# Four quarter transposes for one, and K, Q and V loads issued from POOL instead of SP

## What is computed

```python
def fc(x, z, r):                      # Poincare-ball layer, c = 1
    lam = 2.0 / (1.0 - sum(x * x, -1))
    zn = norm(z, axis=0)
    v = 2 * zn * arcsinh(lam * (x @ (z / zn)) * cosh(2 * r) - (lam - 1) * sinh(2 * r))
    w = sinh(v)
    return w / (1 + sqrt(1 + sum(w * w, -1)))

def attn(x):                          # 16 heads of 64
    Q, K, V = fc(x, z_q, b_q), fc(x, z_k, b_k), x @ w_v.T + b_v
    return softmax(Q @ K.T / 8) @ V   # per head, 2048 x 2048

def ffn(x):
    xp = shift_by_one_token(x)
    xr, xk = mu_r * x + (1 - mu_r) * xp, mu_k * x + (1 - mu_k) * xp
    return sigmoid(xr @ W_r.T) * (relu(xk @ W_k.T) ** 2 @ W_v.T)

x = x + layernorm(attn(layernorm(x)))
x = x + layernorm(ffn(layernorm(x)))
```

## Time and profile before

| | |
|---|---|
| time, median of 2 runs | 3289.42 us (3283.85 to 3295.0) |
| the profiled execution | 3304.93 us, span 3303.1 us on core 2 |
| PE busy | 1878.3 us (57%) |
| ACT busy | 1684.9 us (51%) |
| DVE busy | 1453.6 us (44%) |
| POOL busy | 163.0 us (5%) |
| DMA transposes | 40, all on SP, median 6.7 us from issue to landing |
| K, Q and V loads in attention | 192, all on SP |

### The profile page before, as it was taken

One profiled execution on the slowest core, in us unless ns is written; L12 is line 12 of the kernel. 1 busy time (PEld: TensorE's weight loads), 2 busy tenths in 40 slices (PEclk: granted clock), 3 DMA queues, 4 the chain that ended last, 5 costly groups with the idle time before them and its releaser, 6 DMA issues.

```text
span 3303.1 us, 27750 instructions; the slowest of 8 cores (3266.8 to 3303.1 us)
## 1 busy us (share of the span) xinstructions
PE 1878.3 (57%) x7360; PEld 559.8 (17%) x7360; DVE 1453.6 (44%) x2455; ACT 1684.9 (51%) x1721; POOL 163.0 (5%) x256
## 2 busy tenths in 40 slices
PE   0272462277777787770507354416777978878614
PEld 0130120011122121120203121101111212212101
DVE  2255554211544636527434555440145273363474
ACT  0144645477666766751102653656777467466410
POOL 0000011000000000000000011010000000000000
PEclk9985786589899899895758776668987877878856
DMA  5512123522413314312252122063232142241111
GB/s 75 120 51 45 36 48 59 110 71 53 100 44 88 89 30 109 82 28 51 36 118 74 35 58 51 19 109 80 61 84 69 39 112 55 54 120 47 43 35 39
DMA packets 321561, 217.08 MB, mean 66 GB/s; under 512 B 271872, under 2 KB 280320, under 8 KB 321408
## 3 DMA queue, kind: packets, MB, share of 16 engines
q1 hardware_dynamic: 283264, 109.86, 15.0%
q0 software_dynamic: 38144, 105.45, 13.2%
HBM read 169.03 MB, written 42.21 MB: 64 GB/s over the span
## 4 chain that ended last, share of the span: by engine, by line
ACT 33%; PE 28%; DVE 21%; DMA 9%; issue 7%; DVEq 1%; ACTq 1%; SPq 0%; POOL 0%; POOLq 0%
ACT pool L1095 18%; PE p_attA L1039 4%; DMA pool<-pool 4%; PE psc L1070 3%; PE psc L942 3%; PE p_attB L1047 3%; PE psc L641 3%; PE psc L917 3%; PE psc L678 3%; DVE dump L371 2%; DVE dump L368 2%; ACT pool L533 2%; ACT pool L536 2%; ACT pool L506 2%; ACT pool L509 2%
## 5 line engine op out<-in xcount | busy, mean ns | idle before, releaser
L1095 ACT ACTIVATE pool<-psc 128x1024 bf16<-128x1024 f32 x1024 | 1048.9, 1024 | 538.3 <-PE psc L1077 469.9
L1039 PE MATMUL p_attA<-pool 128*128 128x512 bf16 x1024 | 434.4, 424 | 377.8 <-ACT pool L1095 212.9
L1070 PE MATMUL psc<-pool 64*128 64x512 bf16 x1024 | 428.7, 429 | 46.8 <-DMA pool<-s_vaug 46.8
L1047 PE MATMUL p_attB<-pool 128*128 128x512 bf16 x1024 | 441.7, 431 | 0.0
L1077 PE MATMUL psc<-pool 64*128 64x512 bf16 x1024 | 428.6, 429 | 0.0
L1100 DVE CAST pool<-p_attA 1x512 bf16<-1x512 f32 x64 | 43.8, 685 | 824.8 <-PE p_attB L1047 803.8
L678 PE MATMUL psc<-w_sb,pool 128*128 128x512 bf16 x512 | 141.5, 441 | 287.4 <-DVE pool L693 287.4
L892 PE MATMUL psc<-pool,w_sb 128*128 128x512 bf16 x512 | 128.1, 410 | 190.5 <-DVE pool L877 185.9
L1039 PEld LDWEIGHTS p_attA<-pool 128*128 128x128 bf16 x1024 | 99.6, 97 | 714.6 <-issue 714.6
L457 PE MATMUL psc<-dump,ones_bf 128*128 128x512 bf16 x64 | 35.0, 572 | 286.9 <-DVE dump L451 286.9
L1070 PEld LDWEIGHTS psc<-pool 64*128 64x128 bf16 x1024 | 91.3, 94 | 540.4 <-issue 540.4
(11 more groups left out here) (129 smaller groups left out, 2437.4 us busy)
## 6 DMA issues: line engine op xcount, KB each, us to landing
pool<-s_vaug SPq DMA_DIRECT2D x64, 520.0 KB, 5.1
pool<-s_kfm SPq DMA_DIRECT2D x64, 512.0 KB, 3.4
pool<-x POOLq DMA_DIRECT2D x8, 2048.0 KB, 8.6
pool<-x POOLq DMA_DIRECT2D x32, 512.0 KB, 3.6
out<-pool POOLq DMA_DIRECT2D x32, 512.0 KB, 3.0
s_vaug<-pool POOLq DMA_DIRECT2D x32, 260.0 KB, 2.3
s_qfm<-pool POOLq DMA_DIRECT2D x32, 256.0 KB, 4.8
s_kfm<-pool POOLq DMA_DIRECT2D x32, 256.0 KB, 4.6
```

What stands on the lines that cost most here:

```text
L1039: T(lambda t, c=c, po=po, vof=vof: t.matmul(p_attA[:, :], vsl[:, vof:vof + 128], PT[:, po:po + 512], start=(c == 0), stop=(c == 15), skip_ ...
L1047: tk = T(lambda t, c=c, po=po, vof=vof: t.matmul(p_attB[:, :], vsl[:, vof + 65:vof + 193], PT[:, po + 512:po + 1024], start=(c == 0), stop ...
L1070: T(lambda t, kof=kof, qof=qof, reg=reg: t.matmul(psc[:, reg:reg + 512], Ksl[0:64, kof:kof + 128], Qsl[0:64, qof:qof + QB], start=True, st ...
L1095: lambda s, reg=reg, po=po: s.activation(PT[:, po:po + 1024], psc[:, reg:reg + 1024], AF.Exp, scale=0.125),
```

## The change

Each big DMA transpose is issued as four, one for each tile of 128 tokens (1024 columns of the source). In the production head and in `emit_bndC` each quarter waits for its own normalised tile; the others wait for what the one transpose waited for. The transpose of the denominators is issued as four of 128 columns. Readers wait for the last of the four, as they waited for the one. The three loads of `emit_loads` are emitted with `G` (POOL) instead of `Y` (SP), with the same waits, semaphores and place in the program.

```diff
--- before.py
+++ after.py
@@ -431,11 +431,15 @@
                     ALU.mult, ALU.add),
                     waits=[tk_ln, pc.get("xtm_free_%d" % par)], inc=1))
             tS_ln = p.last["s"]
-            tk_xf_all = Y(lambda y, xnf=xnf, xntm=xntm:
-                          y.dma_start_transpose(
-                r3(xnf[:, :]), r3(xntm[:, :])),
-                waits=[tk_xn[3], pc["xnf_free"][par]], inc=16,
-                sem="y_xp")
+            tk_xf = []
+            for tt in range(4):
+                tk_xf.append(Y(lambda y, tt=tt, xnf=xnf, xntm=xntm:
+                               y.dma_start_transpose(
+                    r3(xnf[:, tt * D:(tt + 1) * D]),
+                    r3(xntm[:, tt * D:(tt + 1) * D])),
+                    waits=[tk_xn[tt], pc["xnf_free"][par]], inc=16,
+                    sem="y_xp"))
+            tk_xf_all = tk_xf[-1]
             pc["xtm_free_%d" % par] = tk_xf_all
             return {"xf_all": tk_xf_all, "par": par, "base": base,
                     "xnf": xnf, "tk_xn3": tk_xn[3], "tS_ln": tS_ln}
@@ -769,18 +773,23 @@
                 waits=[("g_rc", p.cnt["g_rc"]), cy.get("rcp")],
                 inc=16, sem="y_dn")
             cy["dn"] = tk_dn
-            tk_xa = Y(lambda y, afm=attn_fm2[bnd["qb"] % 2]:
-                      y.dma_start_transpose(
-                r3(attn_tm[:, :]), r3(afm[:, :])),
-                waits=[bnd["evac7"], cy["x1stt"], cy["of_free"]],
-                inc=16, sem="y_xp")
-            cy["afm_free"][bnd["qb"] % 2] = tk_xa
-            tk_dt = Y(lambda y: y.dma_start_transpose(
-                den_tm[:, :].rearrange("p (b t) -> p b t", t=16),
-                den_sb[0:16, :].rearrange("p (b t) -> p b t", t=128)),
-                waits=[tk_dn], inc=16, sem="y_xp")
-            bnd["xa"] = tk_xa
-            bnd["dt"] = tk_dt
+            tk_xa = []
+            for tt in range(4):
+                tk_xa.append(Y(lambda y, tt=tt, afm=attn_fm2[bnd["qb"] % 2]:
+                               y.dma_start_transpose(
+                    r3(attn_tm[:, tt * D:(tt + 1) * D]),
+                    r3(afm[:, tt * D:(tt + 1) * D])),
+                    waits=[bnd["evac7"], cy["x1stt"], cy["of_free"]],
+                    inc=16, sem="y_xp"))
+            cy["afm_free"][bnd["qb"] % 2] = tk_xa[-1]
+            tk_dt = []
+            for tt in range(4):
+                tk_dt.append(Y(lambda y, tt=tt: y.dma_start_transpose(
+                    den_tm[:, tt * 16:(tt + 1) * 16],
+                    den_sb[0:16, tt * 128:(tt + 1) * 128]),
+                    waits=[tk_dn], inc=16, sem="y_xp"))
+            bnd["xa"] = tk_xa[-1]
+            bnd["dt"] = tk_dt[-1]
 
         def emit_bndA_v(bnd):
             tk_rcp = V(lambda v: v.reciprocal(rc_tm[:], den_tm[:]),
@@ -834,11 +843,14 @@
                     lncol("inv", tt), lncol("nminv", tt),
                     ALU.mult, ALU.add),
                     waits=[tfin3, cy["x1ntm_free"]], inc=1))
-            tk_xnf = Y(lambda y: y.dma_start_transpose(
-                r3(x1n_fm[:, :]), r3(x1n_tm[:, :])),
-                waits=[tk_x1n[3], cy["v2"]], inc=16, sem="y_xp")
-            cy["x1ntm_free"] = tk_xnf
-            bnd["xnf_all"] = tk_xnf
+            tk_xnf = []
+            for tt in range(4):
+                tk_xnf.append(Y(lambda y, tt=tt: y.dma_start_transpose(
+                    r3(x1n_fm[:, tt * D:(tt + 1) * D]),
+                    r3(x1n_tm[:, tt * D:(tt + 1) * D])),
+                    waits=[tk_x1n[tt], cy["v2"]], inc=16, sem="y_xp"))
+            cy["x1ntm_free"] = tk_xnf[-1]
+            bnd["xnf_all"] = tk_xnf[-1]
 
         def emit_bndD(bnd):
             tk_xnf_all = bnd["xnf_all"]
@@ -960,14 +972,17 @@
             bnd["of_last"] = tk_of[-1]
 
         def emit_ffn2(bnd):
-            tk_ot = Y(lambda y: y.dma_start_transpose(
-                r3(of_tm[:, :]), r3(of_fm[:, :])),
-                waits=[bnd["of_last"], cy["of_free"], cy["x1stt"]],
-                inc=16, sem="y_xp")
-            cy["ofx"] = tk_ot
+            tk_ot = []
+            for tt in range(4):
+                tk_ot.append(Y(lambda y, tt=tt: y.dma_start_transpose(
+                    r3(of_tm[:, tt * D:(tt + 1) * D]),
+                    r3(of_fm[:, tt * D:(tt + 1) * D])),
+                    waits=[bnd["of_last"], cy["of_free"], cy["x1stt"]],
+                    inc=16, sem="y_xp"))
+            cy["ofx"] = tk_ot[-1]
             bnd["tV4"] = lnv_red(
                 lambda tt: of_tm[:, tt * D:(tt + 1) * D],
-                [tk_ot] * 4, alt=True)
+                [tk_ot[-1]] * 4, alt=True)
 
         def emit_ffn3(bnd):
             tS4 = lnv_inv(bnd["tV4"], alt=True)
@@ -1009,14 +1024,14 @@
                 sname = "y_l%d" % sl
                 wk = [tk_qkl[pr - 2] if pr >= 2 else cy["qkl"][sl]]
                 wv_ = [tk_pv[pr - 2] if pr >= 2 else cy["pv"][sl]]
-                Y(lambda y, pr=pr, sl=sl: y.dma_start(
+                G(lambda g, pr=pr, sl=sl: g.dma_start(
                     out=Ksl[:, sl * SEQ:(sl + 1) * SEQ],
                     in_=s_kfm[pr, :, :]), waits=wk, inc=16, sem=sname)
-                Y(lambda y, pr=pr, sl=sl, base=base: y.dma_start(
+                G(lambda g, pr=pr, sl=sl, base=base: g.dma_start(
                     out=Qsl[:, sl * QB:(sl + 1) * QB],
                     in_=s_qfm[pr, :, base:base + QB]), waits=wk,
                   inc=16, sem=sname)
-                tk = Y(lambda y, pr=pr, sl=sl: y.dma_start(
+                tk = G(lambda g, pr=pr, sl=sl: g.dma_start(
                     out=vsl[:, sl * 2144:sl * 2144 + 2080].rearrange(
                         "p (k x) -> p k x", k=16),
                     in_=s_vaug[:, :, 130 * pr:130 * (pr + 1)].rearrange(
```

## The result

| | us, median | ratio to before, 95% interval |
|---|---|---|
| before | 3280.43 | |
| the changed kernel | 3421.11 | 1.0426 (1.0397 to 1.0454) |

The median of before is now one over 10 runs. The medians are over all executions; the ratio leaves out those in which the cores of one die ran at a lower granted clock and took longer. The change costs 4.3%, 140 us on 3280. The forecast was 3423, and its sum 133 us. As the experiments show, two of its terms were wrong by some 40 us each, in opposite directions.

The account below looks back on a forecast made before the run. No single engine owned the chain; ScalarE's exponentials paced attention, and query-block borders mattered. Load stalls and quartering terms summed to 133 us, which on the median of 3289.4 gave 3423; own range 3400 to 3445, wider 3362 to 3462.

Parts of the forecast that it names:

- The hold at the border: At four borders between query blocks, loads on POOL stand behind four output stores that wait for VectorE; 20.0 us lost each.
- V lands 6.0 us after its issue: V load issued from POOL: lands in 6.0 us, against 5.1 from SP, with 1.3 us of issue.
- 4 x 20.0 + 14.3: Load stalls: 20.0 us at each of four full borders, 7.1 after query block 0 in both sequences, together 14.3.
- The starts of attention, 1.8 for both: At each sequence's attention start TensorE waits for V, which lands 0.9 us later from POOL; 1.8 for both.
- Quarters of the same trigger, +3.35 each: Four quarters waiting for one event can't start early; 8.2 us of issue instead of 4.82, 3.35 more.
- The term of 37 us: Quartering the transposes on SP: a fixed cost of 1.12 us for each quarter, 37 us altogether.
- The rival with free quarters: Quartered transposes have no fixed cost, so the sum is 80 instead of 133 us, 3370; chance 0.15.
- Early starts, +0.65: Quarters each waiting for their own normalised tile (L435, L837) end 0.65 us later, not a gain; 1.3 and 2.6 counted.
- Inside the pairs: Within a query block, loads on POOL have some 22 us to land, so they cost nothing.
- this rival: VectorE hinders POOL: V issue 5 us longer, x load 3 us late six times, +18, 3441; 0.13 with slow V landing.
- POOL lets no load pass: Loads on POOL wait behind open stores; the rival let ready loads pass, giving 3340, chance 0.05.
- The clock gives some back: Rival: 20 us of rest restores the granted clock, up to 10 us at each of three blocks, 3393; chance 0.03.

Follow-up runs that it names:

- pre_first: The changed kernel with the loads of the next block's two slots emitted ahead of the output stores; 1.0231 of the kernel before.
- hold_x: The changed kernel with the attention output's transposes at a border also waiting until both slots' loads have landed; 1.0328 of the kernel before.
- q_only: The changed kernel with K, Q and V loads back on SP, so only the transposes are quartered; 0.9998 of the kernel before.
- in_pool: The kernel before, whole transposes, with only the loads for pairs 2 to 7 of each query block on POOL; 0.9988 of the kernel before.
- sp_pre: The changed kernel with the loads at query-block borders issued from SP, those inside a block still from POOL; 1.0055 of the kernel before.
- pool_only: The kernel before with its K, Q and V loads moved to POOL and transposes left whole; 1.0564 of the kernel before.

## Why the prediction was right, step by step

- *The hold at the border*: right in place, mechanism and start. The last output store ends 13.0 us after the denominators' store, and K follows at once. pre_first takes it away and gives back 64 us.
- *V lands 6.0 us after its issue*: right as a median (6.0; issue 1.19, forecast 1.3), too small where it counts. At the first full border it was 8.3 without transposes (hold_x) and 10.0 with them, and after block 0 16.2 (TensorE's first scores at 837.52, V's issue at 821.37). The step that failed is the one that costed the transfer alone and called L773 and L778 "hidden by the new stall". No engine on the path waits for them, but they travel with the loads for which TensorE waits. This put the borders at 139 instead of 94 (4 x 20.0 + 14.3).
- *A restart at the lower clock* was no term of the sum. From first scores to third exponential it is 3.74 us at the first full border, where the forecast had 2.45, so 1.3 us there, inside those 139.
- *The starts of attention, 1.8 for both*: right. TensorE's waits for V there are 24.49 and 24.25 us, before 23.55 and 23.27: 1.9.
- *Quarters of the same trigger, +3.35 each*: wrong. A line through two rows took the small transpose's 1.18 us for a fixed cost; four quarters take 5.4. Where VectorE waits for the FFN output (L368) at the first full border, it waits 7.5 us in q_only, 6.9 before: 0.6 more. The term of 37 us, early starts included, measured 0 (-10 to +8 by q_only's interval). The rival with free quarters, put at 0.15, had this half right. Four small ones are issued in 5.0 us, one in 1.2: 3.8 more, forecast 3.35. In the changed kernel VectorE waits for them only in the tails (26.4 us in two waits), so they are indeed hidden at the borders; in q_only, without that cover, they cost 7.6 us at the four.
- *Early starts, +0.65*: wrong in sign. By the measured quarter, 1.3 x 4 - 2.69 - 4.8 is -2.3 a place, and VectorE's two waits (L451 and L856 before) fall from 29.4 us to 19.2 in q_only and 18.9 in the changed kernel.
- *Inside the pairs*: nothing in the time, shown by in_pool with whole transposes; beside quarters sp_pre leaves 18 us open. The V issue took 1.17 to 1.69 us in all 64 cases of the changed kernel (forecast 1.3), so VectorE did not draw it out. The Trainium skill (SBUF — State Buffer, "Who interferes with whom") says that a VectorE instruction in a two-port mode blocks GpSimd, and the prediction's estimate with that page's example was some 5 us more for a V issue. No issue here shows that; whether a VectorE instruction beside one ran in such a mode, the traces don't tell. The x tiles did come later, as this rival said (23.4 us of waiting in the changed kernel, 17.7 before), but with other POOL issues in front of them that needs no slow issue.
- *POOL lets no load pass*: the rival of 0.05 is out; K's issue stood right behind the last output store's.
- *The clock gives some back*: no sign of it. The blocks between the borders take as long as before (1544.9 and 1548.0 us).

Both errors came from one place, a duration taken from one row with another's conditions, and they cancelled: +45 and -37, so 133 became 141. The forecast also stood on a median of 3289.4 over two runs; on the 3280.4 over ten its sum gives 3413. That the total was right to a few us is luck; the sign and the rough size are not, since the hold was read from the order of two queues.

## What to carry to other kernels
Before moving a DMA to another queue, list what stands in front of it there at the moment when it is urgent, and what that waits for. Then ask what else is in flight then: one queue had kept transposes and loads apart, two don't, and both sides get slower. Splitting a transfer pays where its first part can be issued or read early. Loads with a pair's length of slack could be moved at no cost in time here (in_pool), but look at what then stands behind them.

## What the runs showed of the hardware
- A DMA transpose and plain loads in flight together slow each other. A whole transpose of 4.8 us took 10.7 beside the loads (pool_only) and 29 beside 4 MB of weights (before); V loads of 6.0 us (median) took up to 18.5. With the wait for the loads (hold_x), four quarters are issued in 5.3 us again instead of 13.3, and the longest V load is 11.1.
- The issue of a transpose from SP took some 1.2 us at least: 1 block of 16 x 128 and 64 blocks take 1.2 and 1.3 (q_only).
- After 10 to 37 us of rest (hold_x, pool_only) TensorE's first scores take 0.6 instead of 0.4 us; the granted clock was 0.50 in the one such window read above.
